# Two-layer graph network on one core: how the cosine threshold gets its norms

## The reference, cut to what matters

```python
h = jnp.maximum(_layernorm(x, axis=-1), 0.0)            # 128 graphs, 128 rows, 512
m = h @ map_w.T + map_b
sem = m.reshape(b, s, 8, 64).transpose(0, 2, 1, 3)
norm = jnp.maximum(jnp.linalg.norm(sem, axis=-1, keepdims=True), 1e-8)
n = sem / norm
cos = jnp.einsum('bhsd,bhtd->bhst', n, n)
cos_adj = (cos > 0.1)                                    # and not masked
p_attn = softmax(scores)                                 # scores from q, k of m
adj_h = cos_adj * p_attn                                 # 8 heads x 128 x 128 for each graph
Ax = einsum(adj_h, sem_h); denom = adj_h.sum(-1) + 1.0   # and on to the residual and layer 1
```

## Time and profile before

| | us |
|---|---|
| median of 3 runs | 2518.39 (2517.58 to 2520.62) |
| the profiled execution | 2518.42 |
| its span | 2516.6 |

### The profile page before, as it was taken

How to read it: one execution, slowest core, us unless ns; L and a number is a source line. 1 busy time by engine, 2 the same in 40 slices (tenths; PEclk the granted TensorE clock), 3 DMA queues, 4 the chain that set the end, 5 groups by cost and what they waited for, 6 DMA issues and landing times.

```text
span 2516.6 us, 77531 instructions
## 1 busy us (share of the span) xinstructions
PE 2480.3 (99%) x30008; PEld 1985.3 (79%) x30008; DVE 2016.4 (80%) x3490; ACT 1742.1 (69%) x4528; POOL 1998.7 (79%) x2330
## 2 busy tenths in 40 slices
PE   8899999999999999999999999999999999999997
PEld 6777877878878878778778788788788787787785
DVE  6888888888788787887888887887877878878876
ACT  5676676676676676766766766766767667667665
POOL 4788888888888888888788888788878888887875
PEclk9999999999999999999999999999999999999999
DMA  5566575566665666656655656556666556565642
GB/s 153 94 124 115 115 130 112 114 126 113 124 114 119 126 113 124 126 113 120 126 113 118 122 116 121 118 115 127 115 121 126 113 120 130 113 116 126 117 88 75
DMA packets 820078, 296.37 MB, mean 118 GB/s; under 512 B 761984, under 2 KB 769664, under 8 KB 819712
## 3 DMA queue, kind: packets, MB, share of 16 engines
q1 hardware_dynamic: 819712, 291.41, 59.2%
HBM read 75.80 MB, written 33.55 MB: 43 GB/s over the span
## 4 chain that ended last, share of the span: by engine, by line
PE 94%; DVE 2%; ACT 1%; issue 1%; POOL 1%; DMA 0%; SPq 0%; POOLq 0%; DVEq 0%; ACTq 0%
PE unit_ps L1875 26%; PE unit_ps L2063 26%; PE unit_ps L1889 25%; PE s_ps L1899 4%; PE s_ps L1959 4%; PE c_ps L1899 3%; PE unit_ps L2035 2%; PE unit_ps L1899 2%; PE c_ps L1932 1%; PE unit_ps L1970 1%; ACT e_ec L926 0%; DVE e_ec L1267 0%; DVE qk_sb L1303 0%; DVE x L1429 0%; PE unit_ps L1829 0%
## 5 line engine op out<-in xcount | busy, mean ns | idle before, releaser
L926 ACT ACTIVATE e_ec<-e_ec,neg_mx 128x128 f32<-128x128 f32 x1008 | 389.9, 388 | 4.1
L2063 PE MATMUL unit_ps<-m_hl,w_q_hi 128*128 128x256 f16 x2048 | 356.6, 273 | 0.0
L2063 PE MATMUL unit_ps<-m_hl,w_k_hi 128*128 128x256 f16 x2048 | 355.6, 272 | 0.8 <-DVE qk_sb L1303 0.7
L1022 ACT ACTIVATE qk_hl<-qk_sb 128x512 f16<-128x512 f32 x256 | 153.4, 622 | 288.0 <-DVE qk_sb L1303 288.0
L1875 PE MATMUL unit_ps<-h_t,w_m_hi 128*128 128x256 f16 x2048 | 342.4, 274 | 2.2 <-DVE qk_sb L1303 1.2
L1889 PE MATMUL unit_ps<-w_v_hi,h_t 128*128 128x512 f16 x1024 | 325.1, 379 | 0.0
L1875 PE MATMUL unit_ps<-h_t,w_m_lo 128*128 128x256 f16 x1024 | 280.5, 274 | 0.0
L720 POOL TENSOR_TENSOR e_ec<-e_ec 128x1024 f16<-128x1024 f32 x126 | 269.0, 2135 | 2.1 <-ACT e_ec L956 2.1
L715 POOL TENSOR_TENSOR p_hl<-p_sb,p_hl 128x512 f16<-128x512 f32 x128 | 148.7, 1162 | 146.1 <-ACT p_hl L949 146.1
L2063 PE MATMUL unit_ps<-m_hl,w_q_lo 128*128 128x256 f16 x1024 | 237.5, 273 | 0.0
L2063 PE MATMUL unit_ps<-m_hl,w_k_lo 128*128 128x256 f16 x1024 | 237.3, 272 | 0.0
(11 more groups left out here) (285 smaller groups left out, 7513.7 us busy)
## 6 DMA issues: line engine op xcount, KB each, us to landing
xa<-in_x_dram SPq DMA_DIRECT2D x128, 256.0 KB, 3.4
x<-in_x_dram SPq DMA_DIRECT2D x128, 256.0 KB, 2.9
out_dram<-x SPq DMA_DIRECT2D x128, 256.0 KB, 2.4
h_t<-h_hl SPq DMA_TRANSPOSE x254, 3.4
ec_t<-e_ec SPq DMA_TRANSPOSE x252, 3.2
adj_in<-in_adj_dram SPq DMA_DIRECT2D x128, 16.0 KB, 2.1
p_t<-p_hl SPq DMA_TRANSPOSE x126, 3.3
o_t<-o_hl SPq DMA_TRANSPOSE x124, 3.5
```

Source lines behind the costliest of these rows:

```text
L926: ins = nc.scalar.activation(e[:, h, :], e[:, h, :], ACT.Exp, bias=neg[:, h:h + 1], scale=SCALE, accum_out=sums[:, h:h + 1])
L1022: nc.scalar.activation(dst[:, 0, c, :], src[:, c, :], ACT.Copy).then_inc(done, 1)
L2063: ins = nc.tensor.matmul(ps[:, c % 2 * 2 * P:(c % 2 + 1) * 2 * P], w[a][:, i, c * P:(c + 1) * P], parts[:, b, i, :], start=n == 0, stop=n ...
```

## The change

The norms no longer go through TensorE. POOL's `norm_rows` stops after the power. SP writes the 128 x 16 norms to DRAM (`keep_norms`) and reads them back to every partition, one transfer of 512 KB for each of the two graphs (`spread_norms`), into `norm_n`, laid out as row by head. In each slot POOL multiplies the 1024 spread norms by the partition's own (`threshold`). DVE's `gate` becomes two instructions: `above` compares `c_ps` with `norm_n` and writes ones and zeros over it, and `gate` multiplies the exponentials with these. Both walk `norm_n` head by head, so that one element lies 8 floats behind the one before. The two turning matmuls of a pair, the two subtracting ones of a slot, and DVE's copies to `norm_t` and `norm_r` are gone.

```diff
@@ UNITS and LATE_UNITS
-     ("nt", 1, 1), ("lk", -3, 2), ("wo", -5, 3)),
+     ("lk", -3, 2), ("wo", -5, 3)),
...
@@ tiles
-        norm_parts = sb("norm_parts", [P, P + 2 * H], F16)
-        norm_t = sb("norm_t", [P, P], F16)
-        norm_r = sb("norm_r", [P, 2, C, P], F16)
...
+        norm_d = nc.dram_tensor("norm_d", (2, P, H), F32).ap()
+        norm_n = sb("norm_n", [P, 2, P, H])
...
@@ SP
+            def keep_norms(s):
...
+                if s.has(1):
+                    sp.wait_ge(norm_done, s.at(lambda t: (t + 1) // 2 + 1))
...
+                        wait(sp, norm_in[g], s.at(lambda t: 16 * ((t + 1) // 2)))
...
+                    sp.dma_start(norm_d.rearrange("g n h -> n g h"),
+                                 norm[:, :].rearrange("p (g h) -> p g h", g=2)).then_inc(norm_kept, 16)
+
+            def spread_norms(s):
...
+                if s.has(1):
+                    wait(sp, ec_done, s.at(lambda t: t + 1))
...
+                    sp.wait_ge(norm_kept, s.at(lambda t: 16 * ((t + 1) // 2 + 1)))
+                    for g in range(2):
+                        sp.dma_start(norm_n[:, g].rearrange("p n h -> p (n h)"),
+                                     norm_d[g].rearrange("(a n) h -> a (n h)", a=1).broadcast_to([P, P * H])).then_inc(norm_in[g], 16)
...
@@ SP, odd slots
                     turn_e(s, 0, e_hi)
+                    keep_norms(s)
+                    spread_norms(s)
                     turn_e(s, 1, e_lo)
...
@@ POOL
                     pool.wait_ge(unit_out[u.bank], u.before + 1)
+                    wait(pool, norm_kept, s.at(lambda t: 16 * ((t + 1) // 2)))
+                    wait(pool, threshold_done, s.at(lambda t: t + 1))
                     nc.gpsimd.tensor_tensor(norm[:, :], sq_sum[:, :], plus_half[:, :], ALU.pow).then_inc(norm_done, 1)
...
-                    nc.gpsimd.tensor_copy(parts[:, :, 1:4, :], rows.unsqueeze(2).broadcast_to([P, 2, 3, 2 * C])).then_inc(norm_split, 1)
...
+            def threshold(s):
+
+                if s.has(0):
+                    g = s.n % 2
+                    pool.wait_ge(norm_in[g], s.at(lambda t: 16 * (t // 2 + 1)))
+                    pool.wait_ge(norm_done, s.at(lambda t: t // 2 + 1))
+                    nc.gpsimd.tensor_tensor(norm_n[:, g], norm_n[:, g],
+                                            norm[:, g * H:(g + 1) * H].unsqueeze(1).broadcast_to([P, P, H]),
+                                            ALU.mult).then_inc(threshold_done, 1)
...
@@ DVE
+            def above(s):
+                if s.has(0):
+                    dve.wait_ge(c_full, s.at(lambda t: t + 1))
+                    dve.wait_ge(threshold_done, s.at(lambda t: t + 1))
+                    least = norm_n[:, s.n % 2].rearrange("p n h -> p h n")
+                    nc.vector.tensor_tensor(least, c_ps[:, :, :].rearrange("p a (b n) -> p (a b) n", b=4), least,
+                                            ALU.is_gt).then_inc(passed, 1)
...
-                    nc.vector.scalar_tensor_tensor(
-                        out=e_of(s), in0=c_ps[:, :, :].rearrange("p a (b n) -> p (a b) n", b=4),
-                        scalar=0.0, in1=e_of(s), op0=ALU.is_gt,
-                        op1=ALU.mult).then_inc(ec_done, 1)
+                    dve.wait_ge(passed, s.at(lambda t: t + 1))
+                    nc.vector.tensor_tensor(e_of(s), e_of(s), norm_n[:, s.n % 2].rearrange("p n h -> p h n"),
+                                            ALU.mult).then_inc(ec_done, 1)
...
@@ PE
             def cosines(s):
...
-                    wait(pe, ec_done, s.at(lambda t: t))
+                    wait(pe, passed, s.at(lambda t: t))
...
-                    for a in range(2):
-                        r = slice(a * DK, (a + 1) * DK)
-                        ins = nc.tensor.matmul(c_ps[:, a, :], norm_t[r, :], norm_r[r, s.n % 2].rearrange("p c n -> p (c n)"),
-                                               start=False, stop=True)
```

More of the change, by code:

```diff
@@ L395, in build @@
         norm_done = sem("norm_done")
-        norm_split = sem("norm_split")
+        norm_kept = sem("norm_kept")
+        norm_in = [sem(f"norm_in{i}") for i in range(2)]
+        threshold_done = sem("threshold_done")
+        passed = sem("passed")
         masked = sem("masked")
@@ L630, in _ @@
             turn_e(z, 0, e_hi)
+            keep_norms(z)
+            spread_norms(z)
             turn_e(z, 1, e_lo)
@@ L815, in slot @@
                     block_mask(s)
+                    threshold(s)
                     x_lower(s)
@@ L876, in _ @@
             block_mask(z)
+            threshold(z)
             o1_lower(z, 5)
@@ L886, in _ @@
             h1_lower(a)
+            threshold(a)
+            threshold(b)
             v_lower(a)
@@ L1482, in first_slot @@
                 x_stats(s)
+                above(s)
                 gate(s)
@@ L1745, in _ @@
             o1_rows(z, 5)
+            above(z)
             q_features(z, 1)
@@ L1755, in _ @@
             x1_stats(z)
-            threshold_rows(z)
             lqk_lower(z, "lq", lq_hl, LQ, 0)
             scores_mask(a)
+            above(a)
             scores_mask(b)
@@ L1763, in _ @@
             x1_stats(a)
+            above(b)
             gate(b)
@@ L1891, in rows, with row_pairs @@
                 return ins
-            def row_pairs(outs, mv, st, cols, last=True):
+            def row_pairs(outs, mv, st, cols):
                 for c in range(len(outs[0])):
@@ L1899, in row_pairs @@
                             ins = nc.tensor.matmul(outs[half][c], st[r, a, c, cols], mv[r, b, c, cols],
-                                                   start=n == 0 and (last or c == 0), stop=last and n == 2)
+                                                   start=n == 0, stop=n == 2)
                 return ins
@@ L1923, in cosines @@
                 if s.has(0):
-                    wait(pe, ec_done, s.at(lambda t: t))
+                    wait(pe, passed, s.at(lambda t: t))
                     parts = m_hl[:, s.n // 2 % 2]
                     row_pairs([[c_ps[:, a, c * P:(c + 1) * P] for c in range(C)] for a in range(2)], parts, parts,
-                              columns(s.n % 2), last=False)
-                    u = s.unit("nt", back=1 + s.n % 2)
-                    pe.wait_ge(unit_out[u.bank], u.before + 1)
-                    for a in range(2):
-                        r = slice(a * DK, (a + 1) * DK)
-                        ins = nc.tensor.matmul(c_ps[:, a, :], norm_t[r, :], norm_r[r, s.n % 2].rearrange("p c n -> p (c n)"),
-                                               start=False, stop=True)
-                    ins.then_inc(c_full, 1)
+                              columns(s.n % 2)).then_inc(c_full, 1)
             def l1_scores(s):
@@ L1967, in norms @@
                     for g in range(2):
-                        out = ps[:, 0:2 * H].rearrange("p (a g c) -> p g a c", a=2, g=2)[:, g]
+                        out = ps[:, 0:2 * H].rearrange("p (g a c) -> p g a c", a=2, g=2)[:, g]
                         for n, (c, part) in enumerate((c, part) for c in range(C) for part in range(2)):
```

42 lines of the change are left out of this document (6 added, 36 removed), and 2 rows, old and new, of the table LATE_UNITS.

## The result

| | us | span | against the kernel before |
|---|---|---|---|
| before, beside it | 2517.98 (2515.93 to 2520.62) | 2516.6 | |
| changed | 2772.79 (2772.23 to 2776.75) | 2771.3 | 1.1014, 95% interval 1.1001 to 1.1027 |

Slower by 255 us; 2720 was forecast, in a range from 2570 to 2800. The page: the granted clock in 40 slices, and the chain that ended last.

What follows compares the result with a forecast made beforehand. GpSimd was to replace TensorE as the bound: 37.26 us a pair plus two gate holds of 2.2 gives 41.66, 3.31 over 38.35; times 62 pairs, 205 us on 2518.4 makes 2724, rounded to 2720, range 2570 to 2800.

Steps and rivals of the forecast that it cites:

- TensorE to GpSimd as the bound: Per pair of slots: the bound moves from TensorE, 38.35 us before and 37.80 after, to GpSimd at 41.66.
- the unavoidable one: GpSimd's 0.96 us wait a pair before `h1_lower`, for ACT's two steps on `shift`; it cannot be filled.
- GpSimd's products: Two new GpSimd multiplications of 1024 elements a pair, 2.35 us each, 4.70 us a pair; bounds 2.14 and 2.60.
- The steps: DVE's gate reads `norm_n` 32 bytes apart; taken as 2.2 us, twice the contiguous hold, since single accesses are not hidden.
- The hold: The gate reads two SBUF tiles and so locks GpSimd for its own length, 2.2 us, twice a pair.
- Rival 1: Steps cost DVE nothing, hold 1.1 us: GpSimd still binds at 39.46 us a pair, 2587 us; chance 0.22.
- The DMAs at nothing: Writing the norms and reading them back by DMA is hidden behind GpSimd's other work and costs nothing.
- The window of 9 us against a way of 7: Some 9 us from power to the next even slot's `threshold`; the norms' write and reads need 7 us.
- TensorE's gain: Dropping the turning and subtracting matmuls saves TensorE 0.55 us a pair, 35 us over 64 pairs, hidden under GpSimd.
- Rival 3: Gates fall into GpSimd's waits and hold nobody; TensorE stays the bound, 2483 us; chance 0.08.
- The sum: GpSimd 37.26 + 2 x 2.2 = 41.66 us a pair, 3.31 more than 38.35; 205 us over 62 pairs.
- holds nobody: `above` on DVE reads PSUM and one tile, so it does not lock GpSimd.

Runs made afterwards that it cites:

- e4_fill: The changed kernel with 27 more matmuls in each odd slot, into columns nobody reads, filling TensorE's gap: 2721.9 us, 1.0807 of the kernel before.
- e7: The changed kernel with the gate reading PSUM and `above` moved behind `q_features 1` in odd slots: 2553.0 us, 1.0136 of the kernel before.
- f10: The changed kernel with the gate from PSUM, `above` behind `q_features 1` and `o1_rows 4` ahead of the gate in odd slots: 2507.5 us, 0.9955 of before.
- e8: The changed kernel with the gate reading two contiguous SBUF tiles and `above` behind `q_features 1` in odd slots: 2599.9 us, 1.0328 of before.
- f6_small: The changed kernel with each broadcast read of norms cut to one row, most of the threshold left out: 2771.9 us, 1.1009 of before.
- e1_gate_psum: The changed kernel, but `above` writes its result into the cosines' PSUM banks and the gate reads it there: 2678.8 us, 1.0640 of before.
- e5: The changed kernel with `above` one place later in odd slots, behind `q_features 1`: 2735.5 us, 1.0858 of the kernel before.
- e2: The changed kernel, but `above` writes to its own tile, so the gate reads two contiguous SBUF tiles: 2698.9 us, 1.0716 of before.

## Why the prediction was right, and where it was off

**TensorE to GpSimd as the bound: right.** e4_fill shows GpSimd alone, with no wait but the unavoidable one. In the changed kernel itself GpSimd waited 2.1 us a pair, not 1. DVE stayed behind it, 35.4 us a pair for the 36.6 forecast.

**GpSimd's products: right.** 2.35 us forecast, 2.36 measured. Its own time without the lock was forecast as 36.3 us (37.26 less the 0.96), and is 36.9 in e7 and 36.5 in f10 (37.80 less 14.3 us of waits in eleven pairs), 0.2 to 0.6 us more. Which instructions make up the difference is not shown.

**The steps: right. The hold: too high.** A hold of 2.2 us a gate was taken, 4.4 a pair. The gate is 2.05 to 2.08 us long, but GpSimd's own time rose by 3.4 us for two of them, 1.7 each. This 1.0 us too much and the 0.6 too little above partly cancel, and to that extent the forecast of 41.66 us a pair was lucky. `above` and gate take 1.98 to 2.03 ns for a column of 1024, and so the trace agrees with the table in the Trainium skill (Vector Engine (DVE) Microarchitecture Reference, section Measured stream behaviour on trn2), which has 1.7 to 2.5 for single-element hops. Rival 1, a free step, is out. e8 is that rival built on purpose: 39.35 us a pair, where it was priced at 39.46, though at 2599.9 us and not at 2587.

**The DMAs at nothing: right**, by f6_small. The window of 9 us against a way of 7 was 10.9 us in the pair shown.

**TensorE's gain, 0.55 us a pair: a little high,** 0.44 in f10. Rival 3 needed holds under 0.3 us; f10 takes them away altogether and so comes out faster, but at 2507 and not 2483, because the ramps take 18.5 us of the loop's 25.5.

**The sum.** 41.66 us a pair were forecast where GpSimd alone sets it, 41.27 came (e4). The growth, 3.31, was against 38.35; the true one is 41.27 - 38.24 = 3.03, 62 x 0.28 = 17 us less. That would have made 2707. Two terms were missing from the sum:

- 0.82 us a pair, 51 us, for TensorE's gap and the clock behind it. The prediction said that TensorE would have gaps, and gave them no price because its gain was hidden under GpSimd's sum. It also said that `above` "reads PSUM and one tile and holds nobody": true of the lock, but `above` waits for the product, and behind it on DVE's list stands `q_features 1`, for which TensorE waits. What is queued behind the new wait was the step that failed. Half clock then made TensorE late, and through ACT it gave GpSimd a wait that it did not have.
- About 16 us outside these pairs (e4: 203.5 us above before, of which 62 x 3.03 = 188 in pairs). 8.5 of them lie behind the last power, where e4 takes 84.2 us to its end and the kernel before 75.7; the rest I did not assign.

2724 - 17 + 51 + 16 = 2774, and 2773 was measured. This sum closes because its last two terms are read from e4 and the result; it confirms nothing by itself.

## What to carry to other kernels

Moving an operation from a full engine to one with room pays only if the new operands do not bring the two into each other's way: a DVE instruction with both inputs in SBUF took 0.8 of its own length from GpSimd here when that was busy, and with its operand in a PSUM bank, whose next use could wait, GpSimd's own time was back at 36.9 us. A new wait is to be priced by what stands behind it on the engine's list; here the order of three instructions on DVE was worth 171 us (e1_gate_psum to f10_psum_order). And where TensorE gets a gap close to the bound, half clock behind it is to be kept in the range as a possibility: here it came behind most of the gaps in some runs and behind none in others.

## What the runs showed of the hardware that I had not expected

- TensorE's clock was granted at half after gaps of 2.5 to 3.4 us in this kernel, in two pairs of three, and not in the third with the same gap of 2.48 us. The length of the gap alone does not decide it: in e1 the clock fell behind gaps of 1.66 us, in e8 it held behind all those of 1.5 in the loop, and in e5 behind one of 3.62. What does decide is not shown. Filling the gap with matmuls that nobody reads made the kernel 51 us faster.
- A step of 32 bytes on one SBUF operand gives 2.03 us for 1024 columns, beside a contiguous PSUM operand, whether only the read is stepped (e1, e2) or the write as well (the changed kernel).
- 2048 pieces of 4 bytes take 11.5 us to DRAM, 256 of 32 bytes for the same 8 KB 1.7 us.
